# Perceiver block on one core: values in one piece, row transposes ahead of the probabilities' transposes, statistics half a tile earlier, filler products of ones

## The reference

```python
x = x + xattn(layernorm(x), ctx, ctx)      # 16 heads of 16, 64 queries on 256 keys, biases
x = x + attn(layernorm(x))                 # 16 heads, causal over 64 rows
x = x + ffn(layernorm(x))                  # silu(gate) * up, then down; ternary weights, 8-bit activations

# xattn
q = queries @ Wq.T + bq;  k = keys @ Wk.T + bk;  v = values @ Wv.T + bv
attn = softmax(einsum('blhe,bshe->bhls', q, k) * E ** -0.5)
out = einsum('bhls,bshe->blhe', attn, v) @ Wo.T + bo
```

## Time and profile before

| | before |
|---|---|
| median of 3 runs | 918.96 us |
| profiled execution | 916.78 us |
| its span, first to last instruction | 915.0 us |
| mean granted TensorE clock | 0.997 |
| TensorE busy | 876.1 us (96%) |
| VectorE busy | 758.4 us (83%) |
| ScalarE busy | 695.8 us (76%) |
| GpSimd busy | 431.2 us (47%) |
| DMA | 31.86 MB, 35 GB/s |

### The profile page before, as it was taken

The page is one execution under the profiler, slowest core; times in us unless marked ns, Lnnn a source line. Parts: engine busy times, 40 slices in busy tenths (PEclk is TensorE's granted clock), DMA queues, the critical chain, the costliest instruction groups (busy, mean ns, idle before and its releaser), DMA issues.

```text
span 915.0 us, 28319 instructions
## 1 busy us (share of the span) xinstructions
PE 876.1 (96%) x9666; PEld 732.9 (80%) x9666; DVE 758.4 (83%) x1587; ACT 695.8 (76%) x2046; POOL 431.2 (47%) x643
## 2 busy tenths in 40 slices
PE   6999999999999999999999988999999998899997
PEld 5888988888888888888988976887878775566664
DVE  5878878888888888877887777988888887999996
ACT  4787887776777777778777765777777767899996
POOL 3333334233333333333443226666666662777775
PEclk9999999999999999999999999999999999999999
DMA  6222111110111011111111100000000000001001
GB/s 181 96 90 80 41 46 29 42 49 30 40 46 40 29 46 40 36 39 40 46 29 40 34 2 1 3 1 1 1 0 0 1 2 2 24 30 35 29 32 39
DMA packets 31637, 31.86 MB, mean 35 GB/s; under 512 B 3280, under 2 KB 30800, under 8 KB 31568
## 3 DMA queue, kind: packets, MB, share of 16 engines
q1 hardware_dynamic: 30448, 30.47, 10.9%
q10 hardware_dynamic: 1120, 0.59, 0.2%
HBM read 26.86 MB, written 4.19 MB: 34 GB/s over the span
## 4 chain that ended last, share of the span: by engine, by line
PE 76%; ACT 12%; issue 5%; DVE 4%; POOL 2%; DMA 0%; ACTq 0%; POOLq 0%; SPq 0%; DVEq 0%
PE psum L342 11%; PE psum L297 9%; PE psum L329 9%; PE psum L312 9%; PE psum L368 6%; PE psum L665 4%; ACT probs L1017 4%; PE psum L703 3%; PE psum L377 3%; PE psum L714 3%; PE psum L284 3%; ACT probs L503 3%; PE psum L750 2%; PE psum L684 2%; PE psum L350 2%
## 5 line engine op out<-in xcount | busy, mean ns | idle before, releaser
L503 ACT ACTIVATE probs<-psum,nmax 128x256 f32<-128x256 f32 x512 | 237.3, 488 | 63.1 <-DVE nmax L460 62.3
L460 DVE TENSOR_REDUCE nmax<-psum 128x2 f32<-128x512 f32 x256 | 158.9, 682 | 24.3 <-PE psum L329 23.6
L511 POOL TENSOR_TENSOR rstd<-vare,minus_half 128x1 f32<-128x1 f32 x96 | 53.1, 553 | 153.8 <-DVE vare L398 151.3
L342 PE MATMUL psum<-id_sb,probs 128*128 128x128 f32 x1024 | 124.6, 273 | 0.5 <-ACT probs L503 0.5
L527 POOL TENSOR_TENSOR cl<-c_sb,ch 128x512 fp32r<-128x512 f32 x64 | 81.6, 1275 | 78.8 <-ACT ch L478 78.8
L342 PEld LDWEIGHTS psum<-id_sb,probs 128*128 128x128 f32 x1024 | 113.0, 140 | 3.4 <-ACT probs L503 2.8
L484 ACT ACTIVATE probsT<-psum 128x512 f32<-128x512 f32 x160 | 89.3, 603 | 30.7 <-PE psum L342 30.5
L503 ACT ACTIVATION_READ_ACCUMULATOR probs<-psum,nmax 128x1 f32 x512 | 112.6, 220 | 0.0
L534 POOL TENSOR_TENSOR rm<-rinv,hm_sb 128x256 f32<-128x256 f32 x64 | 39.7, 620 | 120.6 <-DVE rinv L437 120.6
L329 PE MATMUL psum<-k_sb,qb 32*128 32x256 f32 x1024 | 88.8, 400 | 3.8 <-DVE k_sb L413 1.8
L329 PEld LDWEIGHTS psum<-k_sb,qb 32*128 32x128 f32 x1024 | 62.2, 184 | 15.3 <-issue 10.8
(11 more groups left out here) (141 smaller groups left out, 2338.9 us busy)
## 6 DMA issues: line engine op xcount, KB each, us to landing
c_sb<-in_ctx_t SPq DMA_DIRECT2D x64, 256.0 KB, 2.7
x_sb<-in_x SPq DMA_DIRECT2D x32, 128.0 KB, 2.4
out<-y_sb SPq DMA_DIRECT2D x32, 128.0 KB, 1.7
w_all<-in_w_gate SPq DMA_DIRECT2D x1, 1024.0 KB, 6.4
w_all<-in_w_up SPq DMA_DIRECT2D x1, 1024.0 KB, 5.1
w_all<-in_w_down SPq DMA_DIRECT2D x1, 1024.0 KB, 6.6
wqkv_sb<-in_w_qkv SPq DMA_DIRECT2D x1, 768.0 KB, 5.7
wk_sb<-in_wk ACTq DMA_DIRECT2D x1, 256.0 KB, 3.8
```

The lines of the kernel that those rows point to most:

```text
L342: last = nc.tensor.transpose(sp[g][:, c:c + P], probs[:, 2 * g + u, kh * P:(kh + 1) * P], id_sb[:])
L460: nc.vector.tensor_reduce(nmax[:, 2 * g:2 * g + 2], sp[g].rearrange("p (u s) -> p u s", u=2), AX.X, ALU.max, negate=True).then_inc(max_don ...
L503: nc.scalar.activation(probs[:, j, :], sp[g][:, u * S:(u + 1) * S], ACT.Exp, bias=nmax[:, j:j + 1], accum_out=rsum[:, j:j + 1]).then_inc(e ...
L511: nc.gpsimd.tensor_tensor(rstd[:], vare[:], minus_half[:], ALU.pow).then_inc(ln.rstd_done, 1)
```

## The change

There are five edits, all in the cross-attention.

1. TensorE computes both key halves of V for half 1 in one piece, ahead of the transposes of the probabilities of half 0. Before, the second key half stood behind the projection.
2. The two transposes of the rows of tile t + 2 (`pe_xt`) move from behind that to ahead of the probabilities' transposes. They wait for `op_done` of the last tile's second half in place of `y_ev`; the projection waits for `x1h_done`; the product with V of half 0 waits for `y_ev` in every tile from 1 on. ScalarE's `act_xt` moves ahead of `act_pt` accordingly.
3. VectorE does `dve_xn` right behind `dve_o`, and `dve_y` behind both evictions (`dve_pt` 0 and 2), not between them.
4. VectorE's statistics of tile t + 3 stand half a tile earlier than those of the next body did, between `dve_k` and `dve_v` of half 0 of tile t + 1. In body 0 those of tile 2 stay where they were.
5. TensorE multiplies `ones` by `ones` eight times before its first transposes and four times behind them, into a bank that is overwritten later.

```diff
@@ pe_xt
-                pe.wait_ge(y_ev, t - 2)
+                pe.wait_ge(op_done, (t - 2) * 2)
@@ pe_pv
-            elif s == 0:
+            if s == 0 and (not isinstance(t, int) or t > 0):
                 pe.wait_ge(y_ev, t)
@@ pe_out
+            if turned is not None:
+                pe.wait_ge(x1h_done, turned)
@@ TensorE, opening
+                pe.wait_ge(const_set, 2)
+                for i in range(8):
+                    nc.tensor.matmul(sp[0][:, 0:P], ones[:], ones[:], start=True, stop=True)
                 pe.wait_ge(id_in, 16)
                 pe_xt(pe, 0, xt_ps)
+                for i in range(4):
+                    nc.tensor.matmul(sp[0][:, 0:P], ones[:], ones[:], start=True, stop=True)
@@ TensorE, body
                     pe_k(pe, t, 1)
-                    pe_v(pe, t, 1, (0,))
+                    pe_v(pe, t, 1)
+                    if ahead2:
+                        pe_xt(pe, t + 2, xt_ps)
                     pe_transpose(pe, t, 0)
                     if not first:
-                        pe_out(pe, t - 1)
-                    pe_v(pe, t, 1, (1,))
-                    if ahead2:
-                        pe_xt(pe, t + 2, xt_ps)
+                        pe_out(pe, t - 1, t + 3 if ahead2 else None)
                     pe_scores(pe, t, 1, n, j)
@@ VectorE, body
                     if not first:
                         dve_o(v, t - 1, 1)
+                    if first:
+                        dve_stats(v, LN1, t + 2, x_sb[j][:], (x_in[j], (n + 2) * 16))
                     if ahead2:
-                        dve_stats(v, LN1, t + 2, x_sb[j][:], (x_in[j], (n + 2) * 16))
+                        dve_xn(v, LN1, t + 2, x_sb[j][:], xt_mm)
                     dve_k(v, t, 1)
...
                     dve_k(v, t + 1, 0)
+                    if ahead3:
+                        dve_stats(v, LN1, t + 3, x_sb[1 - j][:], (x_in[1 - j], (n + 2 + j) * 16))
                     dve_v(v, t + 1, 0)
                     dve_max(v, t + 1, 0)
@@ ScalarE, body
-                    act_pt(a, t, 0)
                     if ahead2:
                         act_xt(a, t + 2, n + 1, j, xt_ps)
+                    act_pt(a, t, 0)
```

More of the change, by code:

```diff
@@ L372, in pe_pv, with pe_out @@
             last.then_inc(pv_mm, 1)
-        def pe_out(pe, t):
+        def pe_out(pe, t, turned=None):
             pe.wait_ge(o_ev, t * 2 + 2)
+            if turned is not None:
+                pe.wait_ge(x1h_done, turned)
             for k in range(KT):
@@ L1321, in _, with body @@
                 dve_max(v, 0, 0)
-                def body(t, n, j, first=False, scale=False, piece=None, ahead2=True):
+                def body(t, n, j, first=False, scale=False, piece=None, ahead2=True, ahead3=True):
                     if not first:
                         dve_o(v, t - 1, 1)
+                    if first:
+                        dve_stats(v, LN1, t + 2, x_sb[j][:], (x_in[j], (n + 2) * 16))
                     if ahead2:
-                        dve_stats(v, LN1, t + 2, x_sb[j][:], (x_in[j], (n + 2) * 16))
+                        dve_xn(v, LN1, t + 2, x_sb[j][:], xt_mm)
                     dve_k(v, t, 1)
                     dve_inverse(v, t, 0)
-                    dve_pt(v, t, 0, (0,))
-                    if ahead2:
-                        dve_xn(v, LN1, t + 2, x_sb[j][:], xt_mm)
+                    dve_pt(v, t, 0, (0, 2))
                     if not first:
                         dve_y(v, t - 1)
-                    dve_pt(v, t, 0, (2,))
                     if piece is not None:
@@ L1364, in _ @@
                 body(21, 10, 1)
-                with v.Fori(11, NT // 2 - 1) as n:
+                with v.Fori(11, NT // 2 - 2) as n:
                     body(n * 2, n, 0)
                     body(n * 2 + 1, n, 1)
-                body(NT - 2, NT // 2 - 1, 0, ahead2=False)
+                body(NT - 4, NT // 2 - 2, 0)
+                body(NT - 3, NT // 2 - 2, 1, ahead3=False)
+                body(NT - 2, NT // 2 - 1, 0, ahead2=False, ahead3=False)
                 t = NT - 1
```

## The result

The changed kernel takes 924.93 us in the median of four runs (924.14 to 926.02), against 918.98 (917.99 to 919.92) before: a ratio of 1.0073, 95% interval 1.0059 to 1.0087. It is 6 us slower. The profiled execution has a span of 922.9 us, 7.9 longer than before; 2 us of that belong to that execution of before, which was 2.2 under its median.

A forecast was written before the change was run, and what follows sets the result against it. TensorE's list was taken as the bound, matched in even tiles by the ring; -0.8 + 2.8 - 1.6 + 1.0 - 0.1 + 0.5 = +1.8 us gave 918.6 profiled, 920.8 median, range 914 to 924.5.

The forecast's parts named there:

- With a piece: 0.10 + 0.35 + 0.39 + 0.75 = 1.59: Cross-attention tiles with an FFN weight piece: VectorE's maxima start 1.59 us behind the scores' first load, 0.42 later.
- The piece term: Six pairs of cross-attention tiles with FFN weight pieces: +0.42 and +0.05 a pair, +2.8 us in all.
- the signs that the prediction named for being wrong: Tiles with pieces shrink, the projection is less than 0.9 us ahead of the scores, or Q is not sooner.
- Tiles without pieces: Nine pairs of cross-attention tiles without FFN weight pieces: -0.09 us a pair, -0.8 us in all.
- the ring: Cross-attention cycle of scores, nmax, exponentials, probsT evictions and next scores: in even tiles as long as TensorE's own list.
- The seam of 1.07: Cross-attention on TensorE, projection start to scores: 3 x 0.22 + 0.42 = 1.07 us.
- The delay of 0.21 by the statistics: Even cross-attention tiles: statistics moved between dve_k and dve_v make V end at 469.49 against 469.28, +0.21 us.
- The opening: Kernel start: products of ones may let K run at 2.4 GHz, first Q near 11.2, taken as -1.6 us.
- Tile 0: First cross-attention tile: xn waits for POOL's rstd and the scores for the last eviction; taken as +1.0 us.
- rival 1: Cross-attention tiles: the stalls go and no new ones come, about -9 us, 910; chance 0.22.
- Rival 2: VectorE bounds every even tile, with y between evictions and maxima: about +7 us, 926; chance 0.13.
- Rival 3: Little changes but the opening, the rounding being hidden where VectorE waits anyway: 919 us; chance 0.15.

The follow-up runs named there:

- counter-test: Changed kernel with GpSimd's cl for half 0 of the next tile waiting, in tiles 9 to 20, until VectorE's rounding is done: 912.83 us, ratio 0.9943.
- the two runs: Changed kernel without its twelve products of ones: 926.96 us, ratio 1.0097; kernel before with only those products added: 916.6 us, ratio 0.9978.

## Why the prediction was wrong

The place of the loss was right (second halves of tiles with a piece), and so was the direction, this one by luck; the size was not, for two reasons of opposite sign: a collision that cost 12 us, and stretches without pieces that gained 5 us more than forecast.

*The step that failed:* "With a piece: 0.10 + 0.35 + 0.39 + 0.75 = 1.59". The rounding's 0.39 in it measured 1.46 (224.32 to 225.78); the whole was 0.11 + 0.34 + 1.46 + 0.60 = 2.51. The prediction took the rounding's slot from the earlier trace rows as a property of the instruction. It depends on the instruction and on what GpSimd does meanwhile. The prediction said that K would no longer wait for `cl`, so it had `cl` come sooner, but did not ask what `cl` now lies beside. Against the scores' first load, `cl` came 1.01 sooner in tile 12 (0.43 behind it, before 1.44) and the rounding 0.42 later (0.45, before 0.03). The two meet. The piece term, +2.8, measured +12.0: 13.3 in second halves, less 1.3 in first ones. The counter-test splits the 13.3: 12.7 collision, 0.6 the rest. None of the signs that the prediction named for being wrong came up: tiles with pieces grew, the projection is 1.07 ahead of the scores, and Q is sooner. No sign stood for a rounding that gets longer.

The trace of before had the sign of it. At the opening `xn` takes 0.81 us in place of 0.40 to 0.42 and ends 0.15 behind GpSimd's `x1l`; a split of weights takes 0.96 in place of the 0.68 of the next one and ends 0.55 behind GpSimd's `cl`. GpSimd's `rstd`, which comes behind the split, takes 1.01 in place of 0.55:

```profile
5.68 1.27 POOL L527 TENSOR_TENSOR cl<-c_sb,ch 128x512 fp32r<-128x512 f32 x1 [0.98 <-ACT ch L478]
6.54 0.96 DVE L1309 TENSOR_TENSOR wkl<-wk_sb,wkh 128x512 fp32r<-128x512 f32 x1
6.91 1.01 POOL L511 TENSOR_TENSOR rstd<-vare,minus_half 128x1 f32<-128x1 f32 x1
...
7.89 0.72 POOL L517 TENSOR_TENSOR x1l<-xnT,x1h 128x256 fp32r<-128x256 f32 x1
7.95 0.81 DVE L403 TENSOR_SCALAR xn<-x_sb,mv,rstd 128x256 f32<-128x256 f32 x1 [0.45 <-POOL rstd L511]
```

An instruction blocked in this way shows no idle time ahead of it; it only gets longer. The waits' view can't show it, the spread of durations by line does.

The Trainium skill states the rule ("SBUF — State Buffer", Who interferes with whom): VectorE and GpSimd share one pair of SBUF ports as a lock for a whole instruction; a VectorE operation in its two-port mode, and one with two SBUF inputs beside a GpSimd read, contend for it, and the one that comes second stands still; one with at most one SBUF input outside that mode, and a reduction, do not. The runs agree: 1.54 = 1.25 (the rest of `cl`) + 0.29, and 0.94 = 0.64 + 0.30 where less of `cl` is met, and back to 0.48 by moving either party; V, the residual sum and the maxima, which read PSUM, kept their lengths beside `cl`. That it is the ports on which the two meet is the page's word; the runs show only that the rounding does not get on while `cl` runs, and no row shows the mode of the rounding. The prediction left this page out. With it, the place of `cl` beside the rounding would have been a question to put a price on.

*Tiles without pieces*, -0.8 predicted, -5.6 measured. The mechanism was right (y at +0.22, row transposes right behind xn, K's wait gone). Three sizes were off. V's slot is 0.60; the 0.75 of the earlier trace rows held a wait for the scores' result, as I read a step between starts as the cost of the first. With 0.60 the maxima are not late at all (1.16). Second, the gain at the scores was put at 0.1; from the scores to the product with V it was 0.24 (1.31 to 1.07). Third, xn started 0.07 sooner in the half than predicted, and its signal took 0.05, not 0.12. First halves shrank by 0.07 to 0.26 (0.04 predicted), odd second halves by some 0.22 (0.10 predicted), even ones by 0 to 0.13 (0.28 in tile 8), since there the ring of maxima, exponentials and evictions holds, as predicted. The seam of 1.07 was hit with luck: the projection's four loads start within 0.54, not 3 x 0.22 = 0.66, and the step from the last to the scores is 0.52, not 0.42. The delay of 0.21 by the statistics was 0.02.

*The opening*: -1.6 predicted, -1.6 in the profile, 1.7 to 2.2 by the two runs; first Q at 11.17 where 11.2 was said. K's twelve matmuls took 2.59 us before (7.55 to 10.14) and 1.42 after (7.57 to 8.99). The traces' record of the granted clock opens with the full level at 12.38 us before the change and at 6.92 after it and has no entry ahead of that, so that the lower level of K before is read from its pace. *Tile 0*: +1.0 predicted, +0.7. *The end*: +0.4 predicted in all, +0.5 in the profile up to the last wait.

So without the collision the change would have been a gain of some 6 us (the counter-test, with 912.83 against 918.34), by the mechanism of rival 1 and at two thirds of its price of 9; the collision of 12 us made it a 6 us loss. That the direction came out as forecast is luck: what makes the kernel slower, the collision, was not in the forecast, and with V's slot at 0.60 in the fifteen even second halves that it counted (15 x 0.15 = 2.2) its own sum of +1.8 would have been -0.4. Rival 2 (VectorE bounds every even tile) fell: it happened only in tiles with a piece, and not by the seam. Rival 3 fell too.

What stays open: the profiled span grew by 2.3 us behind tile 31's start, of which 0.5 is the longer wait there. In the changed kernel's profile the granted clock is at the lower level twice around the change to self-attention (556.5 to 559.9 and 573.5 to 576.9), in that of before once (565.4 to 568.8). With the ones alone it is there twice too, and that span is 1.2 us longer behind tile 31's start than before, with the same program there. So about 1 us of the 2.3 goes with the second stretch. The rest, 1.0, comes in the FFN, in four steps of 0.24 that lie 33.5 us apart (from 783 us of the trace of before on). All versions built on the changed kernel have such steps, the kernel before and the one with the ones alone don't; their cause was not traced. So the table's sum lies near the medians (+5.95) partly because the profiled execution of before was 2.2 us under its median.

## What to carry to other kernels

When an instruction moves on one engine, follow what it releases through to GpSimd and lay VectorE's and GpSimd's timetables side by side: here a VectorE operation from SBUF to SBUF should run where GpSimd is idle, while those from PSUM ran beside it at their usual length. Look at least, median and most duration of a line before a duration goes into a sum, and take a slot from a place where nothing is waited for. Filler work of a periodic kind (here the weight pieces) belongs into a stretch in which the engine waits anyway, not between a released wait and the ring's next step.

## What the runs showed of the hardware

A VectorE rounding of 128 x 512 float32 in SBUF takes 0.48 us alone, 1.54 when it comes 0.02 us behind a 1.27 us GpSimd subtraction, and 0.94 when it comes 0.62 behind it: it ends 0.29 to 0.30 after the subtraction each time. Going from full-size matmuls to those of 32 rows costs 0.2 to 0.3 us more than going to the next full-size ones: behind the two row transposes 0.37 to the scores and 0.17 to the probabilities' transposes, behind the projection 1.07 to the scores and 0.76 to V. With twelve products of ones from 1.08 us on, K's first products run from 7.57 to 8.99 us, where the same ones took from 7.55 to 10.14.
